# A graph network's attention layers without the unread TensorE products in the last chunks of each layer

## The reference

```
def _gat_layer(x, src, dst, edge_attr_full, W, att, b, ew, eb):
    edge_emb = edge_attr_full @ ew.T + eb
    xw = x @ W
    xj = xw[src] + edge_emb;  xi = xw[dst]            # reshaped to (E, 2, 128)
    alpha = leaky_relu(xi . att_i + xj . att_j, 0.2)
    ea = exp(alpha - segment_max(alpha, dst)[dst])
    alpha = ea / (segment_sum(ea, dst)[dst] + 1e-16)
    return segment_sum(xj * alpha, dst).mean(axis=1) + b
```

## Time and profile before

| | |
|---|---|
| plain runs, median | 4483.73 us (4479.84 to 4488.99) |
| profiled execution | 4464.49 us, of which the span from first to last instruction is 4462.5 |
| mean granted TensorE clock | 0.554 |
| TensorE matmuls | 2643.4 us busy (59%), 13626 recorded |
| VectorE | 1905.6 us busy (43%) |
| ScalarE | 547.7 us busy (12%) |
| GpSimd | 2351.1 us busy (53%), most of it in issuing gathers |
| the chain that ended last | GpSimd 26%, TensorE 19%, "issue" 18%, not attributed 17%, VectorE 14% |

### The profile page before, as it was taken

How to read it: one execution, slowest core, us unless ns; L and a number is a source line. 1 busy time by engine, 2 the same in 40 slices (tenths; PEclk the granted TensorE clock), 3 DMA queues, 4 the chain that set the end, 5 groups by cost and what they waited for, 6 DMA issues and landing times.

```text
span 4462.5 us, 47152 instructions
## 1 busy us (share of the span) xinstructions
PE 2643.4 (59%) x13626; PEld 2108.9 (47%) x13626; DVE 1905.6 (43%) x6874; ACT 547.7 (12%) x2646; POOL 2351.1 (53%) x2611
## 2 busy tenths in 40 slices
PE   7523334246766926666863666692666675467668
PEld 6422233135555615555553555561555554355556
DVE  9701111434444624444453444453444444344445
ACT  0000000111111211111021111112111102111111
POOL 0166665456666256666345666625656635566661
PEclk7555555555555855555575555585555577555558
DMA  3222221312222022222111222202222212122221
GB/s 109 73 48 48 45 48 39 96 42 51 48 54 47 22 76 49 49 47 54 29 62 44 50 50 48 52 20 77 49 49 48 53 33 69 43 51 47 49 47 32
DMA packets 128777, 228.38 MB, mean 51 GB/s; under 512 B 41715, under 2 KB 86167, under 8 KB 127239
## 3 DMA queue, kind: packets, MB, share of 16 engines
q0 software_dynamic: 75104, 156.37, 15.6%
q1 hardware_dynamic: 53414, 69.01, 4.8%
HBM read 211.75 MB, written 13.46 MB: 50 GB/s over the span
## 4 chain that ended last, share of the span: by engine, by line
POOL 26%; PE 19%; issue 18%; another core or an unknown queue 17%; DVE 14%; ACTq 2%; ACT 2%; DVEq 1%; DMA 1%; SPq 0%; POOLq 0%
POOL ring L482 25%; PE bank L704 7%; PE bank L706 4%; PE bank L712 3%; DVE acc L1149 2%; ACTq L526 2%; DVE prod L1027 1%; PE bank L649 1%; DVE acc L998 1%; DVE ring L824 1%; DMA ring<-table,srci 1%; PE bank L774 1%; ACT ai_win L526 1%; DVEq L978 1%
## 5 line engine op out<-in xcount | busy, mean ns | idle before, releaser
L482 POOL DMA_INDIRECT ring<-table,srci x1955 | 1870.9, 957 | 1219.6 <-issue 537.7
L704 PE MATMUL bank<-pw,ring 128*128 128x48 f32 x3910 | 1200.4, 404 | 109.6 <-DMA ring<-table,srci 77.9
L704 PEld LDWEIGHTS bank<-pw,ring 128*128 128x128 f32 x3910 | 944.6, 296 | 261.3 <-issue 144.2
L1149 DVE TENSOR_TENSOR acc<-acc,bank 128x72 f32 x1955 | 448.9, 230 | 1360.2 <-remote 774.1
L706 PE MATMUL bank<-onehot,est 128*36 128x24 f32 x3910 | 600.1, 239 | 0.7 <-issue 0.7
L461 POOL DMA_INDIRECT ring<-table,srci x392 | 373.4, 953 | 378.0 <-DMA table<-ring 201.6
L526 ACT COPY ai_win<-ai_rows 128x48 f32 x1955 | 350.1, 229 | 1437.0 <-issue 1326.1
L706 PEld LDWEIGHTS bank<-onehot,est 128*36 128x36 f32 x3910 | 368.3, 144 | 167.5
L649 PE MATMUL bank<-onehot,ring 128*128 128x24 f32 x784 | 177.2, 388 | 412.5 <-DVE acc L998 255.6
L649 PEld LDWEIGHTS bank<-onehot,ring 128*128 128x128 f32 x784 | 171.1, 330 | 418.7 <-DVE acc L998 226.0
L662 PE MATMUL bank<-identf,alpha 128*56 128x128 f32 (+2 forms) x75 | 29.0, 387 | 480.4 <-DVE alpha L1065 251.8
(11 more groups left out here) (200 smaller groups left out, 2836.9 us busy)
## 6 DMA issues: line engine op xcount, KB each, us to landing
ring<-table,srci POOLq DMA_INDIRECT x2347
ai_rows<-ai_dram SPq DMA_DIRECT2D x10, 1600.0 KB
at<-in_attr SPq DMA_DIRECT2D x65, 224.0 KB
ai_rows<-lo_dram SPq DMA_DIRECT2D x14, 896.0 KB, 4.5
table<-ring SPq DMA_DIRECT2D x25, 325.0 KB, 3.3
table<-ring SPq DMA_DIRECT2D x25, 65.0 KB, 2.4
x_mid<-ring SPq DMA_DIRECT2D x1, 1600.0 KB, 7.0
result<-ring SPq DMA_DIRECT2D x24, 64.0 KB
```

Of the source, the lines that this page charges most:

```text
L482: nc.gpsimd.indirect_dma_start(out=ring[:, slot(t), :], out_offset=None, in_=table, in_offset=bass.IndirectOffsetOnAxis(ap=srci[:, t:t + 1 ...
L704: nc.tensor.matmul(o[:, 0:H * WIN], ring[:, slot(t), 0:D], pw[:, g % 3, k, :, :].rearrange("p h w -> p (h w)"), start=True, stop=True)
L1149: V.tensor_tensor(win, win, grp_sum(g, k).rearrange("p (r w) -> p r w", r=REG), ALU.add)\
```

## The change

All calls of `keep_warm` and the function itself go, and with them the wait in chunk 9 for the last self tile to have left bank 3. Nothing else in the program changes.

```
-            def keep_warm(times):
-                for _ in range(times):
-                    nc.tensor.matmul(bank[3][:, 0:21 * WIN], identf[:, :],
-                                     onehot[:, 0:21, :].rearrange("p t w -> p (t w)"), start=True, stop=True)
-
@@
                         if s_tile_of(c, i) is not None:
                             self_tile(s_tile_of(c, i))
-                        if c == 9 and i == 0:
-                            pe.wait_ge(s_sb, n + NT)
-                        if c == NC - 4 and i == lag(c):
-                            keep_warm(6)
-                        elif c >= NC - 3 or c == NC - 4 and i > lag(c):
-                            keep_warm(1)
                         if more and i == lag(c):
                             chain_alpha(layer, c + 1)
...
                     if more:
-                        if c >= NC - 4:
-                            keep_warm(1)
                         chain_probs(layer, c + 1)
-                        if c >= NC - 4:
-                            keep_warm(2)
```

## The result

Twenty plain runs of each kernel: 4475.55 us before (4443.08 to 4511.08), 4491.83 us after (4482.74 to 4500.86). The medians differ by 16.3 us. The ratio of the runs is 1.0046, 95% interval 1.0025 to 1.0067, which is 20.6 us; it leaves out the one run of the kernel before that counts as slow, 4511.08 us, more than 1.5% above the fastest. So the changed kernel is slower, by 16 to 21 us. Its profiled execution, which is one of the twenty, took 4485.85 us (span 4483.7), 21.4 us over the profiled one of the kernel before.

What follows compares the result with a forecast made beforehand. Gathers and freed slots bound chunk 10, TensorE chunk 12 and the node sums, VectorE the loop. Layer changes of +8.8, -12.4, +8.8, +11.6 and +9.1 gave +26, so 4490 or 4491; the offset's middle made it 4500, range 4472 to 4520.

Steps and rivals of the forecast that it cites:

- the sum: Chunk 11 to the node loop: stage changes added per layer, together +26 us, giving 4490 or 4491 from the profiled execution.
- the term that is easy to overlook: Node sums: the products also keep the clock for work behind them; without them +3.2 us in layer 0.
- The nine calls of chunk 11: Nine of chunk 11's eleven unread-product calls were counted as costing nothing, since signals of finished groups arrive late anyway.
- first rival: Chunk 11: the six products hold up the preceding group's signal; removal saves 33 us more, ending at 4458 to 4477; chance 0.13.
- the pair: The last two calls of chunk 11, lying in the open: removing them saves 1.8 us, chunk 11 becoming 42.3.
- The offset: Whole execution: the profiled execution is 19.2 us below the plain runs' median; two readings weighted equally, middle taken, 4500.
- first reading: Plain runs lost the high clock in one layer more; the kernel without the products has nothing to lose, stays at 4491.
- The price of a lost layer: Chunks 12, 13 and the node sums: losing the high clock costs 17.3+2.6+1.3 = 21 us.
- The second rival: Loop over node tiles: gets its high clock late or never, 9 us per layer, 4536 to 4555; chance 0.07.
- the third: Chunks 12 to 14: tile products hold or regain 2.4 GHz by themselves, 4382 in all; chance 0.04.

## Why the prediction came out

**Right in the mechanism and in each stage.** "I take 0.5 for chunks 12 to 14 and the node sums in every layer" held. What it was taken from shows less than that: layer 1 had a low clock and did not get a high one, which says nothing on whether tile products keep one. That they don't came from the kernel with calls only around the transposes. Chunk 12 was put at 29.3 us and took 29.0, chunk 13 19.1 and 18.6, chunk 14 10.4 and 10.4, node sums 20.8 and 20.6, loop unchanged. From the start of chunk 11 to the end of the loop the layers changed by +8.2, -13.2, +8.1, +11.5 and +8.6 us, where the sum had +8.8, -12.4, +8.8, +11.6 and +9.1: together +23.2 against +26. The rest of the profiled execution changed by -1.8 us. It was taken to stay, and did so only in the sum: nine of the 55 chunks 0 to 10 took some 41.5 us, where one did before, and the others 44.1 for 43.8. The kernel before has eight such chunks in its second trace, so this is not the change. The node sums, the term that is easy to overlook, were 3.0 us in layer 0.

**The nine calls of chunk 11.** Counted at nothing, against the first rival's 33 us. Chunk 11 fell from 44.0 to 42.6, so -1.4 where I had -1.8 for the pair; between the second traces of both kernels, on one chip, it is -1.9 on average. The prediction calls chunk 11 "seven groups at 1.2 GHz" beside a row that says 0.58: the six bring 6.8 us of high level there in layer 0, which it passes over, and which on this kind of chip is worth next to nothing, as the chunk waits for signals. VectorE's wait in chunk 11 is there without any unread product, in the changed kernel's order of time:

```profile
1443.16 1.32 DVE L1134 TENSOR_TENSOR acc<-acc,bank 128x72 f32 x4 [7.13 <-remote]
...
1459.26 1.32 DVE L1134 TENSOR_TENSOR acc<-acc,bank 128x72 f32 x4 [6.22 <-remote]
```

The kernel with calls only from the end of chunk 11 on shows the same from the other side: eight of the eleven gone, chunk 11 at most 0.3 us shorter in four layers of five. The first rival is out. On the second kind of chip the six even pay for themselves.

**The offset.** This is the step that was mis-sized. Of the two readings of the 19.2 us between the profiled execution and the plain runs I took the middle, and so put some 9.6 us into the forecast of 4500 that are not there. A profiled execution is not shorter than others by a constant: that of the changed kernel lies 6.0 us under the median of its twenty, its second one 5.0 over the median of twelve. The first reading was right: 20 runs of the kernel before range over 68 us, those of the changed kernel over 18, and the three that were known (4480 to 4489) happened to lie in the upper half. With the first reading alone the forecast would have been 4491, and 4491.8 was measured. That this is so close is luck: the profiled execution came out 4.6 us under the sum, and the median of the plain runs 6.0 over the profiled execution. The price of a lost layer, 21 us from the earlier trace rows, was 15.5 in the second trace of the kernel before, where its node sums were short. That plain runs differ by none to some four lost layers is an estimate from their mean clocks; which layers they are can't be seen in those.

**The second rival** (the loop gets its clock late) and **the third** (tile products hold it) had 0.07 and 0.04. The loop took 29.3 us in all layers, and the kernel with calls only around the transposes shows the third to be wrong even from a high start.

## What to carry to other kernels

Work whose result nobody reads can be worth its time for what it does to the clock of the work behind it, but look up in which stage and in which executions it does: here the products gained 9 us in a layer when they worked and lost 13 when they didn't, and the mean of that is 0.46%. Before a difference of less than one such event is predicted, ask for more than three plain runs, or count the events by the mean clock of each run and in the profile. Beside a late signal from elsewhere even 6.7 us of extra TensorE work were free here.

## What the runs showed of the hardware

**What lifts and what holds the level.** In these traces the products of 504 columns around the transposes lift it; without the two behind them it stays low in all five layers. Tile products of 48 and 24 columns alone lose it again 3.4 to 6.8 us after the rise; with one 504-column product after every group it holds, with one of 240 it doesn't. In the chunks compared TensorE is busy nearly from end to end. The Trainium skill ("TensorE: Matmul & The Clock Gate", Part 1) says that the level follows how busy the engine has been; here busy time as the profile shows it is no lower where the level was lost (28.80 of 28.80 at 0.57) than where it held (25.45 of 25.80 at 1.00), so it doesn't tell which one you will get.

**Two kinds of chip.** The same kernel takes 4470 us on one and 3710 on the other. The line of VectorE's additions on the page, of the changed kernel (first kind) and of the kernel without the six (second kind): instructions | busy, mean ns | idle before them and what ended most of it.

```profile
L1134 DVE TENSOR_TENSOR acc<-acc,bank 128x72 f32 x1955 | 449.9, 230 | 1367.1 <-remote 763.6
```

```profile
L1149 DVE TENSOR_TENSOR acc<-acc,bank 128x72 f32 x1955 | 449.6, 230 | 700.2 <-PE bank L706 439.7
```

An addition takes 230 ns on both. The idle time before it is 667 us longer on the first kind, most of it released by a signal that the profile can't attribute. The last group of TensorE's that the changed kernel has in chunk 11 of layer 0, with the addition that waits for it, and the same in chunk 10 of the kernel without the six:

```profile
1452.23 0.32 PE L706 MATMUL bank<-onehot,est 128*36 128x24 f32 x2
...
1459.26 1.32 DVE L1134 TENSOR_TENSOR acc<-acc,bank 128x72 f32 x4 [6.22 <-remote]
```

```profile
1224.37 0.32 PE L706 MATMUL bank<-onehot,est 128*36 128x24 f32 x2
...
1224.82 1.31 DVE L1149 TENSOR_TENSOR acc<-acc,bank 128x72 f32 x4 [1.40 <-PE bank L706]
```

On the first kind the addition begins 6.7 us after the recorded end of the group, on the second 0.1 us. Delays of 6 to 8 us are the commonest on the first kind; they come in chunks with gathers and in none without. TensorE's clock is at 0.50 in both cases (on the first kind by the 0.66 us of its products), so its level alone is not what makes the signals late. Chunk 10 takes 41 to 45 us there and some 36.5 on the second kind. What delays the signals is open. Between the second trace of the kernel before (span 4464.7 us) and that without the six (3735.6) lie 729 us, some 35 times the change studied here: 394 in chunks 0 to 10 of the five layers, 112 ahead of the first chunk of layer 0, and some 47 at each of the four passages from a loop's end to the next layer's first chunk. How much of that is late signals isn't shown.
